# Reordering the tail of a fused adaLN, window-attention and mixture-of-experts block on one NeuronCore

## The reference, cut to what matters

```
mod = silu(c) @ wmod                      # sa, ca, ga, sb, cb, gb for each image; |ga|, |gb| >= 0.25
h   = layernorm(x) * (1 + ca) + sa
x   = x + ga * attention(h)               # 16 heads of 128, 8 key heads, rope, 2-tap conv on k and v,
                                          # causal window of 128, then @ W_o
h   = layernorm(x) * (1 + cb) + sb
xn  = w_norm * h / sqrt(mean(h * h) + 1e-6)
probs = softmax(xn @ w_router)            # 32 experts, top 4; an expert takes its first 128 tokens
out = sum over the chosen experts of prob * ((silu(xn @ w_gate[e]) * (xn @ w_up[e])) @ w_down[e])
sh  = (silu(xn @ sw_gate) * (xn @ sw_up)) @ sw_down        # shared expert, 704 hidden features
out = out + sigmoid(xn @ w_shared_gate) * sh
x   = x + gb * (h + out)
```

## Time and profile before

| | us |
|---|---|
| median of 3 runs | 891.35 (891.22 to 895.29) |
| the profiled execution | 889.4 |
| its span, first to last instruction | 887.5 |

### The profile page before, as it was taken

The page is one execution under the profiler, slowest core; times in us unless marked ns, Lnnn a source line. Parts: engine busy times, 40 slices in busy tenths (PEclk is TensorE's granted clock), DMA queues, the critical chain, the costliest instruction groups (busy, mean ns, idle before and its releaser), DMA issues.

```text
span 887.5 us, 12864 instructions
## 1 busy us (share of the span) xinstructions
PE 784.2 (88%) x3978; PEld 638.7 (72%) x3978; DVE 556.0 (63%) x1719; ACT 460.9 (52%) x1153; POOL 429.1 (48%) x370
## 2 busy tenths in 40 slices
PE   3788999999999998999999999967798989867873
PEld 2477888887788887888888878855665666645652
DVE  3298776788776888686878776764323434323554
ACT  4467867677875667875577776634412212101110
POOL 0444454456463786563588655473260000373741
PEclk9989999999999999999999999997799999987987
DMA  8902000000031010004010004083115998352885
GB/s 313 314 1 73 25 1 1 1 1 1 1 108 59 31 49 19 1 1 143 19 36 34 1 1 143 1 254 97 72 48 161 288 274 265 116 152 62 162 103 95
DMA packets 65101, 78.22 MB, mean 88 GB/s; under 512 B 6632, under 2 KB 55797, under 8 KB 65040
## 3 DMA queue, kind: packets, MB, share of 16 engines
q1 hardware_dynamic: 52528, 56.84, 20.5%
q0 software_dynamic: 6144, 12.61, 7.6%
q10 hardware_dynamic: 6368, 8.03, 2.7%
HBM read 56.44 MB, written 25.20 MB: 92 GB/s over the span
## 4 chain that ended last, share of the span: by engine, by line
PE 65%; DVE 8%; issue 7%; ACT 7%; DMA 6%; SPq 4%; POOL 2%; another core or an unknown queue 1%; ACTq 0%; DVEq 0%; POOLq 0%
PE PJ L1187 18%; PE OUT L1284 10%; PE U L1273 5%; PE U L1239 5%; PE U L1262 4%; PE U L1397 4%; PE U L1187 3%; PE U L1238 3%; PE U L1274 2%; DMA wd<-in_dram 2%; PE U L1440 2%; PE OUT L1440 2%; DMA xin<-in_dram 2%; DMA bas<-residual_rows 2%; ACT U L472 1%
## 5 line engine op out<-in xcount | busy, mean ns | idle before, releaser
L677 POOL TENSOR_TENSOR qsw<-qsw,sinT 128x512 f32<-128x512 f32 x96 | 124.6, 1298 | 218.1 <-ACT qsw L459 213.7
L472 ACT ACTIVATE U<-U,nmax 128x128 f32<-128x128 f32 (+1 forms) x256 | 99.0, 387 | 84.1 <-DVE nmax L849 81.4
L1284 PE MATMUL OUT<-wo,oT 128*128 128x256 f32 x512 | 133.7, 385 | 0.0
L849 DVE CUSTOM_DVE_ANT_0 U<-U,mask 128x128 f32<-128x128 f32 (+1 forms) x256 | 86.7, 380 | 74.6 <-PE U L1239 74.0
L774 POOL DMA_INDIRECT gat<-expert_rows,gidx x64 | 62.6, 978 | 139.7 <-DMA expert_rows<-ye 99.4
L1187 PE MATMUL PJ<-hT_hi,w_hi 128*128 128x512 f32 x256 | 112.9, 441 | 0.8 <-issue 0.8
L1187 PE MATMUL PJ<-hT_lo,w_hi 128*128 128x512 f32 x256 | 102.3, 399 | 0.0
L1187 PE MATMUL PJ<-hT_hi,w_lo 128*128 128x512 f32 x256 | 101.8, 398 | 0.0
L859 DVE TENSOR_SCALAR prob<-U,rinv 128x128 f32<-128x128 f32 (+1 forms) x256 | 95.1, 413 | 4.5
L1273 PE MATMUL U<-pT,vN 128*128 128x256 f32 x256 | 79.7, 394 | 19.3 <-ACT pT L480 11.7
L458 ACT ACTIVATE qsw<-PJ 64x512 f32<-64x512 f32 x96 | 57.0, 594 | 72.9 <-PE PJ L1187 69.3
(11 more groups left out here) (175 smaller groups left out, 1677.9 us busy)
## 6 DMA issues: line engine op xcount, KB each, us to landing
wgu<-in_dram SPq DMA_DIRECT2D x32, 352.0 KB
wd<-in_dram SPq DMA_DIRECT2D x16, 352.0 KB
wraw<-in_dram SPq DMA_DIRECT2D x8, 512.0 KB, 14.1
slot_rows<-eq SPq DMA_DIRECT2D x1, 4096.0 KB, 16.0
bcm<-mod_rows SPq DMA_DIRECT2D x8, 512.0 KB, 6.7
xe<-slot_rows SPq DMA_DIRECT2D x16, 256.0 KB, 6.4
expert_rows<-ye ACTq DMA_DIRECT2D x16, 256.0 KB, 6.5
xin<-in_dram SPq DMA_DIRECT2D x4, 512.0 KB, 6.8
```

Of the source, the lines that this page charges most:

```text
L472: last = act.activation(U[n % 3][:, a:z], U[n % 3][:, a:z], ACT.Exp, scale=-1.0, bias=nmax[:, n % 4, j:j + 1], accum_out=rsum[:, n % 4, j: ...
L677: pool.tensor_tensor(pair3(qsw[:, n % NQSW, :]), pair3(qsw[:, n % NQSW, :]), both(sinT[:, :]), ALU.mult).then_inc(t2_done, 1)
L849: last = dve.tensor_tensor_reduce(out=U[n % 3][:, a:z], in0=U[n % 3][:, a:z], in1=mask[:, a:z], scale=-float(HD) ** -0.5, scalar=3.4e38, o ...
L1284: last = pe.matmul(OUT[b][:, t * H:(t + 1) * H], oT[:, n % NOT, t * PN:(t + 1) * PN], wo[:, head, :], start=(head == 0 and t == 0), stop=( ...
```

## The change

1. **Prefix in two matmuls.** `carry` gets one row set per tile. DVE makes `carry[t] = carry[t-1] + chosen[t-1]` in `post_choice`, by three additions that depend on each other, ahead of the signal that PE waits for; `post_prefix` is one matmul with `ones` and one with `tri`, 128 columns each. The reduction over tiles in `post_weights` goes.
2. **Weights split inside the stream.** Each chunk of the attention weights gets a tile of its own, so that the shared weights can lie where the first chunks lay. SP loads them once projection 112 is done (`W_FREE`), behind the loads of pair 3. ACT makes the high part in four pieces at units 20, 24, 26 and 28 of the last 32, DVE the low part at units 20, 28, 29 and 30. The piece of ACT at unit 20 waits for both loads.
3. **Order of the tail.** `gate_up(0, 0)` runs in step 128 of the stream, in banks PJ0 and PJ1 (even slices use these now, odd ones U0 and U1). Shared passes 0 and 1 run whole before the experts, passes 2 and 3 whole behind them, without hardware loops on PE and ACT. `combine` of pair 0 comes after `hidden` of pass 2.
4. **Loads.** The shared inputs have two buffers and all are loaded by SP. The first expert weights wait for slices of pass 0 instead of following the last projection.
5. `post_xhat` waits and takes the reciprocal per image, with ACT's `post_std` of the last pair in two parts.

```diff
-F_EARLY = 3
+W_FREE = NU - UNITS // 2
+SW_PARTS = 4
+SWC = 2 * FS // SW_PARTS
...
+        GU = ((PJ[0], PJ[1]), (U[0], U[1]))
...
@@ SP
+            sp.wait_ge(pj_ps, W_FREE)
+            for n, src in enumerate((sw_gate, sw_up)):
+                sp.dma_start(swraw[:, :, n * FS:(n + 1) * FS], src.rearrange("(c p) f -> p c f", p=PN)).then_inc(ld_sw, 16)
...
+            sp.wait_ge(pj_ps, NU)
+            sp.wait_ge(st_xnt, 32 * 2)
+            shared_inputs(0)
+            shared_inputs(1)
...
             sp.wait_ge(y_ps, 2 * NPAIR)
...
-            pair_stores(NPAIR - 1)
+            for i in range(HALF):
+                sp.wait_ge(sh_ps, i + 2)
+                expert_weights(2 * i, i)
+            pair_stores(LAST)
+            sp.wait_ge(sh_ps, FT)
+            shared_inputs(2)
...
                 slot_rows(2 * i, i)
+            sp.wait_ge(sh_ps, 2 * FT)
+            sp.wait_ge(st_xnt, 32 * NPAIR)
+            shared_inputs(3)
@@ ACT
+                if p == LAST - 1 and l in (20, 24, 26, 28):
+                    shared_high((20, 24, 26, 28).index(l))
+
+            def shared_high(k):
+                act.wait_ge(ld_sw, 32)
+                act.activation(sw_hi[:, :, k * SWC:(k + 1) * SWC], swraw[:, :, k * SWC:(k + 1) * SWC], ACT.Copy).then_inc(sw_hi_done, 1)
...
-            act.wait_ge(ld_sw, 32)
-            act.activation(sw_hi[:, :, :], swraw[:, :, :], ACT.Copy).then_inc(sw_hi_done, 1)
...
-            with act.Fori(1, LAST) as q:
-                shared_inputs(q + 1)
+            for q in range(2, NPAIR):
+                for f in range(FT):
+                    silu_of(q, f)
                 shared_rows(q)
-                for f in range(FT):
-                    silu_of(q + 1, f)
-            shared_rows(LAST)
@@ DVE
+                own(dve.tensor_scalar(chosen[:, :, :], zz2[:, :, 0:E], TAKEN / 2, None, ALU.is_lt))
+                for t in range(1, TT):
+                    last = dve.tensor_tensor(carry[:, t, :], carry[:, t - 1, :], chosen[:, t - 1, :], ALU.add)
+                    if t + 1 < TT:
+                        own(last)
+                last.then_inc(chosen_done, 1)
...
-                own(dve.tensor_reduce(carry[:, 1, :], chosen[:, :, :].rearrange("p t e -> p e t"), AXX, ALU.add))
-                dve.tensor_tensor(carry[:, 0, :], carry[:, 0, :], carry[:, 1, :], ALU.add).then_inc(wsel_done, 1)
+                dve.tensor_tensor(carry[:, 0, :], carry[:, TT - 1, :], chosen[:, TT - 1, :], ALU.add).then_inc(wsel_done, 1)
...
+                if p == LAST - 1 and l in (20, 28, 29, 30):
+                    shared_low((20, 28, 29, 30).index(l))
...
+            for f in range(FT):
+                hidden(2, f)
+            for t in range(TT):
                 combine(0, t)
+            hidden(3, 0)
+            hidden(3, 1)
             combine(1, 0)
+            hidden(3, 2)
+            hidden(3, 3)
+            combine(1, 1)
+            hidden(3, 4)
+            hidden(3, 5)
+            for t in range(2, TT):
                 combine(1, t)
+            for q in range(2, NPAIR):
+                for t in range(TT):
+                    combine(q, t)
@@ PE
-                for t in range(TT):
-                    o = XB[:, 256 + t * E:256 + (t + 1) * E]
-                    pe.matmul(o, ones[:, :], carry[:, 0, :], start=True, stop=False)
-                    for u in range(t):
-                        pe.matmul(o, ones[:, :], chosen[:, u, :], start=False, stop=False)
-                    last = pe.matmul(o, tri[:, :], chosen[:, t, :], start=False, stop=True)
+                pos = XB[:, 256:256 + TT * E]
+                pe.matmul(pos, ones[:, :], carry[:, 0:TT, :].rearrange("p t e -> p (t e)"), start=True, stop=False)
+                last = pe.matmul(pos, tri[:, :], chosen[:, :, :].rearrange("p t e -> p (t e)"), start=False, stop=True)
...
+                if n == NU:
+                    pe.wait_ge(pj_dve, NU)
+                    pe.wait_ge(sw_lo_done, SW_PARTS)
+                    gate_up(0, 0)
...
             pe.wait_ge(ot_done, NU)
+            for f in range(1, 4):
+                gate_up(0, f)
             post_xnt(LAST, 0)
+            gate_up(0, 4)
             post_xnt(LAST, 1)
             post_logits(LAST)
+            gate_up(0, 5)
             post_prefix(LAST)
...
+            for f in range(FT):
                 gate_up(1, f)
+            for t in range(TT):
+                down(1, t)
...
-            for f in range(F_EARLY, FT):
-                gate_up(1, f)
-            with pe.Fori(1, LAST) as q:
+            for q in range(2, NPAIR):
+                for f in range(FT):
+                    gate_up(q, f)
                 for t in range(TT):
                     down(q, t)
-                for f in range(FT):
-                    gate_up(q + 1, f)
```

More of the change, by code:

```diff
@@ L77, in adaln_block @@
         sgate = sb("sgate", [PN, NPAIR, TT])
-        carry = sb("carry", [PN, 2, E])
+        carry = sb("carry", [PN, TT + 1, E])
         att = ExitStack()
@@ L142, in adaln_block @@
         proj_w = ExitStack()
[L143 to L147, removed]
+        w_hi, w_lo, wraw = {}, {}, {}
+        for j in W_ORDER:
+            w_hi[j] = sb(f"w_hi{j}", [PN, HC, WC], F32R, proj_w)
+            raws = ExitStack()
+            wraw[j] = sb(f"wraw{j}", [PN, HC, WC], F32, raws)
+            raws.close()
+            w_lo[j] = sb(f"w_lo{j}", [PN, HC, WC], F32R, proj_w)
         proj_w.close()
         exps = ExitStack()
-        wgu = sb("wgu", [PN, RING, HC, 2 * F], F32, exps)
-        wd = sb("wd", [FH, RING, 2, H], F32, exps)
         sw_hi = sb("sw_hi", [PN, HC, 2 * FS], F32R, exps)
@@ L582, in _ @@
                 hooks(n)
[L584 to L587, removed]
             def silu_of(q, f):
@@ L631, in _ @@
             post_rms(LAST)
-            silu_of(0, 2)
+            silu_of(0, 3)
             post_xnt(LAST, 0)
-            silu_of(0, 3)
+            silu_of(0, 4)
             post_xnt(LAST, 1)
             post_exp(LAST)
-            silu_of(0, 4)
             silu_of(0, 5)
-            shared_inputs(1)
             shared_rows(0)
-            for f in range(F_EARLY):
+            for f in range(FT):
                 silu_of(1, f)
+            shared_rows(1)
             for n in range(RING):
@@ L1085, in _ @@
             hidden(0, 1)
+            hidden(0, 2)
             post_xn(LAST, 0)
             post_xn(LAST, 1)
-            hidden(0, 2)
+            hidden(0, 3)
             post_xnt(LAST, 0)
-            hidden(0, 3)
+            hidden(0, 4)
             post_xnt(LAST, 1)
@@ L1213, in project @@
                 p, l = divmod(m, UNITS)
[L1214 removed]
+                j, at = divmod(head_of(l) * HD, WC)
+                cols = slice(at, at + HD)
                 if l == 0:
@@ L1352, in _, with gate_up, down @@
             last.then_inc(mod_ps, 1)
+            def gate_up(q, f):
+                if f == 0:
+                    pe.wait_ge(ld_xs[q % 2], 32 * (q // 2 + 1))
+                fw = min(PN, FS - f * PN)
+                if f >= 2 or later(q):
+                    pe.wait_ge(hs_done, FT * q + (f - 1))
+                for off, bk in ((0, GU[f % 2][0]), (FS, GU[f % 2][1])):
+                    cols = slice(off + f * PN, off + f * PN + fw)
+                    last = halves(bk[0:fw, :], HC,
+                                  ((lambda c: sw_hi[:, c, cols], lambda c: sw_lo[:, c, cols]),
+                                   (lambda c: xs_hi[:, q % 2, c, :], lambda c: xs_lo[:, q % 2, c, :])))
+                last.then_inc(sh_ps, 1)
+            def down(q, t):
+                if t == 0:
+                    pe.wait_ge(hs_done, FT * (q + 1))
+                if t >= 2 or later(q):
+                    pe.wait_ge(shrow_done, TT * q + (t - 1))
+                for f in range(FT):
+                    fw = min(PN, FS - f * PN)
+                    last = pe.matmul(DN[t % 2][:, 0:H], hs[0:fw, f, t * PN:(t + 1) * PN], swd[0:fw, f, :],
+                                     start=(f == 0), stop=(f == FT - 1))
+                last.then_inc(dn_ps, 1)
             for n in STEPS:
@@ L1461, in _ @@
                 down(0, t)
-            for f in range(F_EARLY):
+            for f in range(FT):
                 gate_up(1, f)
+            for t in range(TT):
+                down(1, t)
             pe.wait_ge(pos_used, NPAIR)
-            pe.wait_ge(shrow_done, TT)
-            pe.wait_ge(hs_done, FT + F_EARLY)
+            pe.wait_ge(shrow_done, 2 * TT)
+            pe.wait_ge(hs_done, 2 * FT)
             for n in range(RING):
```

128 lines of the change are left out of this document (36 added, 92 removed).

## The result

The change makes the kernel slower: 904.4 us (median of 4 runs, 903.3 to 908.8) for 891.3 us, a ratio of 1.0155 (95% interval 1.011 to 1.0199). I had forecast 881. The forecast had -9.5 us there; of the 28.7 us between, 16.1 lie in the tail, 6.6 ahead of the experts and 4.1 at the end of the stream, by the table.

The account below looks back on a forecast made before the run. PE bounds the stream, PE and DMA the experts, POOL's gathers the last 125 us. Terms -7.6 + 11.5 - 6.3 + 12.8 - 18.5 - 1.4 = -9.5 us gave 881 us, 8-in-10 range 868 to 898.

Parts of the forecast that it names:

- The prefix: In the PE-bound stream: two matmuls gain 2.6 us for each of three pairs, -7.6 us (bounds -7.8 and -4).
- Weights split inside the stream: At unit 20 of pair 3: ACT waits for the shared weights' load, making PE late; +11.5 us (bounds +3 and +15).
- End of the stream: At 592 to 600 us: 6.3 of PE's 7.55 us stop goes as expert weights move; -6.3 us (bounds 0 and -7.55).
- the scatters stay: At the end of the stream: expert weights move behind pass 0, scatters remain, with 6.3 of PE's 7.55 us stop gone.
- From there to the experts: Last output to first expert: 21.8 us of PE work added, less what is taken off; +12.8 us (bounds +8 and +16).
- hidden: Before the experts: the last pair's 20.5 us of scatters lie behind PE's work, so PE is the bound.
- The tail: Behind the experts: 3 of POOL's 21.5 us waits stay, -18.5 us (bounds -21.5 and 0); -1.4 us more at the close.
- the loop as the cause: In the tail: hardware loops make ACT's 28.2 us of standing still, which goes with them; straight-running DVE showed no stop.
- ACT's 3 us in straight code: During the scatters: ACT stood still about 3 us in straight code, named as evidence against the loop.
- The first rival: In the tail: gathers, not the loop, stop ACT; the tail keeps 124.5 us, experts end 10.4 later; 901 us, chance 0.20.
- decides once the waits in the tail exceed about 12 us: In the tail: size of POOL's waits above which the first rival decides; the forecast kept 3 us.
- the last 125 us are POOL's: Behind the experts: 64 gathers in 103 us, 21.5 of it waits for DVE's additions; 80.7 us without them.

Follow-up runs that it names:

- e1: Kernel before with only the prefix in two matmuls, three additions on DVE ahead of it: 885.2 us, ratio 0.9951.
- e13: Kernel before with the short prefix and a tiny POOL operation behind each of the 64 gathers; order, loops and split kept: 879.8 us, ratio 0.9866.
- e3: Kernel after with the first piece of the shared weights' split moved from unit 20 to 23 (ACT) and 24 (DVE): 892.5 us, ratio 1.0026.
- e4: Kernel after without the last 8 scatters of pair 2 and all 16 of the last pair: 890.9 us, ratio 1.0000.
- e14: e9 with the tiny POOL operation also behind pair 2's 16 scatters: 862.6 us, ratio 0.9651.
- e11: Kernel after with a tiny POOL operation behind each of the last pair's 16 scatters and each of the 64 gathers: 888.5 us, ratio 0.9978.
- e2: Kernel before with the tail's loops over the shared passes on PE and ACT written out: 891.4 us, ratio 1.0016.
- e8: e3 with all 64 gathers left out, DVE adding zeros in place of the experts' rows: 850.0 us, ratio 0.9545.
- e9: e5 with a tiny POOL operation behind each of the 64 gathers: 861.3 us, ratio 0.9635.
- e5: e3 with the tail's old order, only three slices of pass 1 ahead of the experts, in straight code: 867.9 us, ratio 0.9731.
- e7: e3 with a small POOL operation (128x256) behind each of the last pair's 16 scatters: 886.6 us, ratio 0.9957.
- e6: e3 with DVE's additions of pairs 0 and 1 moved between the slices of passes 2 and 3: 900.8 us, ratio 1.0120.
- e12: e5 with the tiny POOL operation behind every second gather only: 867.3 us, ratio 0.9717.
- e10: e5 with a tiny POOL operation behind each of the last pair's 16 scatters only: 872.8 us, ratio 0.9779.

## Why the prediction was wrong

**The prefix** was right: -7.6 forecast, -9.6 in e1 and -6.5 in e13. What I didn't see is that the gain is partly lost further on.

**Weights split inside the stream** was right: +11.5 forecast (bounds +3 and +15). The kernel after needs 13.6 us more than e1 and 10.4 more than e13 from pair 1 to the last projection, and 10.3 go with the wait (e3).

**End of the stream**: I took PE's 7.55 us stop as bound to the expert weights and the scatters together, and 6.3 us of it as gone with the weights. Without the weights (DMA share 0.24) a stop is still there; DVE has it now:

```profile
608.59 0.42 DVE L875 COPY oT<-U 128x256 f32<-128x256 f32 x1 [8.10 <-remote]
```

Of its 8.1 us 3.9 lie behind PE's last matmul for it (604.7), the rest is waiting for PE. e4 and e14 take it away, e14 in part, by the scatters alone; the stage then takes 22.4 us for 27.1. The step that failed is "the scatters stay" as a cost of nothing.

**From there to the experts**: +12.8 forecast, bounds +8 and +16; +19.4 measured. The sum of PE's work was good: with the scatters spaced it is +11.1 (e11, 73.7 for 62.6, and the 62.6 still have the stops of the kernel before in them). What is missing are 8.4 us (e11) to 11.2 us (e4) of ACT's stops, which I had in sight in the kernel before and left out because the scatters were "hidden". Their duration was hidden; what they do to ACT was not.

**The tail** is where the forecast broke: -18.5 - 1.4 forecast, -3.8 measured. I chose the loop as the cause of ACT's 28.2 us; e2 shows that it isn't, and e8 and e9 that the gathers are. The argument that DVE runs straight code and shows no stop of its own was weak: in the kernel after, at the stream's end, DVE does stop in straight code, for 8.1 us. I had the contrary evidence, ACT's 3 us in straight code, and priced it at 0.20. The Trainium skill (Runtime: NRT & Kernel Launch, Instruction fetch mechanics) says that a taken branch may force an instruction fetch; here the unrolled tail has the same time (ratio 1.0016), so that rule explains none of these stops.

The first rival was right in its mechanism and near in its time (901 us), with its 10.4 us at the experts too small by half and its tail 4 us too long. It said "decides once the waits in the tail exceed about 12 us": POOL waited 16.1.

A deeper error lay under the sum. I had written that the last 125 us are POOL's, and still counted on POOL's waits going when PE's work leaves the tail; I kept 3 us of them, and 16.1 were there. POOL's chain of 64 gathers bounds the tail in both orders: 117.1 and 117.8 us (e5 and e3), and without waits 109.5 and 110.2 us (e9 and e11), with some 20 us of PE's work between the two of each pair. Work moved from there to a stretch that PE bounds is paid in full and earns nothing. The tail came nearest to the forecast's -19.9 us in e11: with the gathers spread out no wait is left, -11.4 us, at a pitch of 1.46 us instead of the 1.26 that I had counted.

## What to carry to other kernels

Before moving an engine's work out of a stretch, ask which engine bounds the stretch; if it is a chain of indirect DMAs on POOL, it gets no shorter. Read a long run of indirect DMAs as a resource that other engines pay for: spread them by a small operation, to the point where the waits go, and look whether they went (they did in e9 and e11, not in e13); the best pitch here was above the fastest (e9, 861.3 us, is the fastest version here; leave the second pass behind the experts). And a wait in program order can cost nearly what it lasts: ACT's 11.2 us for the shared weights cost 10.3 us of the stream; three units later it was free. Last, read a term from more than one trace where you can: the same stretch of the same program differed by 3 us between e1 and e13.

## What the runs showed of the hardware

Indirect DMAs issued by POOL 1.26 to 1.28 us apart stop ACT, in loops and in straight code alike, with idle times of 4 to 18.5 us (the longest in e3), of which 2.2 to 3.9 us can be the ordinary wait for PE (ACT's waits among the spaced scatters of e7). DVE's long idle times mostly follow ACT's: in the kernel after one of 12.4 us ends at 659.84, 0.03 us behind ACT's `silu`. At the stream's end DVE stands by itself, 3.9 us after PE's last matmul for it.

What ends a stop is open. In four places it ends 2.5 to 4.2 us after POOL pauses (664.5 and 667.0, 808.7 and 811.5 in the kernel after; 809.1 and 813.2 in e6; 801.2 and 805.4 in the kernel before). But of ACT's 12 idle times of over 10 us under an unknown releaser or none, among gathers without added operations, seven end before POOL pauses (15.65 us in e5, 17.7 in e1, 14.5 and 16.9 in e6).

How far apart the DMAs must be isn't sharp either. With 1.37 us on average (e12) stops of up to 7.9 us are left, with 1.43 us of up to 5.8 us (e9) and 6.6 us (e13), with 1.46 us among the gathers (e11) none under an unknown releaser, with 1.47 us among the scatters (e10, e11) and with 2.46 us (e7) none. It isn't DMA load: in the expert stage of the kernel after the share is 0.74, and all of ACT's waits there have a known releaser, the longest 4.8 us. It isn't a busy POOL: in the stream it works 90 of 137 us, mostly on additions and products, without such stops. That the gathers delay the loading of ACT's own instructions was not tested. Against it speaks only that the trace of the kernel before has no packet on either of its two instruction queues from 778.5 to 823.9 us, while ACT's stop of 17.0 us ends at 805.4; which engines these queues serve it doesn't say.

The Trainium skill (DMA: Bandwidth & Descriptors, SWDGE vs HWDGE vs iDMA) says that DMAs issued from POOL have their descriptors built by software on GpSimd; it names no cost to other engines, and what inside the chip ACT and DVE wait for stays open: no run here could show it. Whether the same gathers on another queue would do this wasn't tried.
